# Tokens, stacks, probabilities and hidden rings at another place within 128 bytes of SBUF

## What is computed

```python
x = x + 0.5 * ffn(layernorm(x))
x = x + attn(layernorm(x))
x = x + 0.5 * ffn(layernorm(x))

# ffn: a gated layer of 1024 inner units, and 512 experts chosen by product keys
mlp = silu(x @ gate_w) * (x @ up_w) @ down_w
scores, pk = top_k(sx[:, :, None] + sy[:, None, :], 8)      # from top 8 of each of two key sets
ew = silu(x . down_embed[indices]) * softmax(scores)
out = mlp + ew @ up_embed[indices]

# attn: 16 heads of 16 features; q, k, v and o are linear layers with a low-rank update
scores = einsum('bhqd,bhkd->bhqk', q, k) / 4
out = lora_linear(einsum('bhqk,bhkd->bhqd', softmax(scores), v), Wo, ...)
```

## Time and profile before

| | |
|---|---|
| median of 3 runs | 810.65 us (809.98 to 813.35) |
| the profiled execution | 809.31 us, of which its span is 807.5 |
| PE busy | 788.1 us |
| VectorE busy | 659.9 us |
| ScalarE busy | 471.2 us |
| granted TensorE clock | 1.00 of full |

### The profile page before, as it was taken

One profiled execution on the slowest core, in us unless ns is written; L12 is line 12 of the kernel. 1 busy time (PEld: TensorE's weight loads), 2 busy tenths in 40 slices (PEclk: granted clock), 3 DMA queues, 4 the chain that ended last, 5 costly groups with the idle time before them and its releaser, 6 DMA issues.

```text
span 807.5 us, 14439 instructions
## 1 busy us (share of the span) xinstructions
PE 788.1 (98%) x5424; PEld 535.0 (66%) x5424; DVE 659.9 (82%) x1225; ACT 471.2 (58%) x929; POOL 155.4 (19%) x183
## 2 busy tenths in 40 slices
PE   5999999999999999999999999999999999999998
PEld 4778888887876544444444444444487888888886
DVE  5998788687779999999999999995078786775854
ACT  4544333333342699999999999999864342332323
POOL 1661102021111033332222222211100211020200
PEclk9999999999999999999999999999999999999999
DMA  8119000000040332223333222411000000000000
GB/s 286 40 40 409 8 1 2 1 1 0 1 79 14 65 57 41 41 41 93 93 93 94 41 41 43 125 69 68 2 2 0 1 2 27 0 27 1 1 26 27
DMA packets 18645, 40.45 MB, mean 50 GB/s; under 512 B 4688, under 2 KB 12176, under 8 KB 16528
## 3 DMA queue, kind: packets, MB, share of 16 engines
q1 hardware_dynamic: 18384, 39.14, 18.7%
q10 hardware_dynamic: 192, 0.39, 0.2%
HBM read 16.29 MB, written 10.49 MB: 33 GB/s over the span
## 4 chain that ended last, share of the span: by engine, by line
PE 92%; DVE 4%; issue 1%; ACT 1%; POOL 1%; DMA 1%; SPq 0%; DVEq 0%; ACTq 0%; POOLq 0%
PE front_ps L1560 17%; PE front_ps L1543 12%; PE max_ps L1503 9%; PE ffn_out_ps L659 6%; PE ffn_out_ps L661 5%; PE ffn_out_ps L660 5%; PE ffn_gate_ps L48 5%; PE ffn_gate_ps L50 5%; PE ffn_gate_ps L49 5%; PE ffn_up_ps L50 3%; PE ffn_up_ps L48 3%; PE ffn_up_ps L49 3%; PE ffn_mix_ps L643 2%; PE ffn_up_ps L379 1%; PE front_ps L1529 1%
## 5 line engine op out<-in xcount | busy, mean ns | idle before, releaser
L1713 DVE TENSOR_REDUCE maxima<-max_ps 128x1 f32<-128x512 f32 (+1 forms) x384 | 303.2, 859 | 6.3 <-PE max_ps L1503 5.3
L1651 ACT ACTIVATE probs<-front_ps 128x512 f32<-128x512 f32 x512 | 267.0, 598 | 27.1 <-PE front_ps L1543 22.8
L791 ACT ACTIVATE ffn_tanh<-ffn_gate_ps 128x512 f32<-128x512 f32 x96 | 57.5, 599 | 215.2 <-PE ffn_gate_ps L50 215.2
L1560 PE MATMUL front_ps<-probs,values 128*32 128x256 f32 x2048 | 150.1, 388 | 0.5 <-ACT probs L1651 0.4
L1037 DVE SCALAR_TENSOR_TENSOR ffn_gated<-ffn_tanh,ffn_gate_ps 128x512 f32<-128x512 f32 x96 | 65.7, 685 | 72.6 <-ACT ffn_tanh L791 72.6
L1560 PEld LDWEIGHTS front_ps<-probs,values 128*32 128x32 f32 x2048 | 47.0, 108 | 68.0 <-issue 55.6
L1461 POOL TENSOR_TENSOR inverse_sum<-turned,minus_one 128x16 f32<-128x16 f32 x15 | 43.7, 2915 | 241.5 <-ACT turned L1663 241.5
L1543 PE MATMUL front_ps<-q_stack,k_stack 49*128 49x512 f32 x256 | 86.6, 436 | 0.7 <-ACT attn_out L1269 0.7
L1503 PE MATMUL max_ps<-ffn_xlo,ffn_xhi 48*128 48x512 f32 x256 | 87.2, 437 | 0.0
L1543 PE MATMUL front_ps<-ffn_xhi,ffn_xlo 49*128 49x512 f32 x256 | 85.4, 444 | 0.0
L1503 PE MATMUL max_ps<-k_stack,q_stack 48*128 48x512 f32 x256 | 83.4, 447 | 0.0
(11 more groups left out here) (194 smaller groups left out, 1255.6 us busy)
## 6 DMA issues: line engine op xcount, KB each, us to landing
split_weights<-block SPq DMA_DIRECT2D x8, 1024.0 KB, 10.3
block<-split_weights SPq DMA_DIRECT2D x8, 1024.0 KB, 4.9
q_stack<-block SPq DMA_DIRECT2D x48, 64.0 KB, 2.3
ffn_xhi<-block SPq DMA_DIRECT2D x48, 64.0 KB, 2.3
ffn_xlo<-block SPq DMA_DIRECT2D x48, 64.0 KB, 2.3
k_stack<-block SPq DMA_DIRECT2D x42, 64.0 KB, 2.3
x_sb<-in_x SPq DMA_DIRECT2D x4, 512.0 KB, 6.3
out<-x_sb SPq DMA_DIRECT2D x3, 512.0 KB, 2.9
```

The lines of the kernel that those rows point to most:

```text
L1560: mm = pe.matmul(mixed_ps[strip:strip + STRIP, at:at + HALF // 2], values[g % SLOTS][:, kt, j, :], probs[:, (g * KEY_TILES + kt) % PROBS, ...
L1651: act.activation(probs[:, tile % PROBS, j, half * HALF:(half + 1) * HALF], score_ps[:, n % RING, :], ACT.Exp, scale=SCORE_SCALE).then_inc( ...
L1713: v.reduce_max(maxima[:, g % 2, m // 2, m % 2, heads], max_ps[:, m % 2, heads, :], axis=AXIS_X).then_inc(unit_max, 1)
```

## The change

It allocates two tiles that nothing reads or writes: 8 values (32 bytes) ahead of `ffn_xhi`, and in layer 1 alone 16 values (64 bytes) ahead of `hidden`. All that is allocated behind them moves by as much.

```diff
@@ -28,6 +28,8 @@
 CHUNKS = TOKENS // CHUNK
+HIDDEN_OFFSET = 16
+HALVES_OFFSET = 8
 CT = CHUNK // P
@@ -413,6 +415,8 @@
         full = sb("full", [P, 2, KT, PAIR_TILES, P])
+        if not first:
+            sb("beside_hidden", [P, HIDDEN_OFFSET])
         hidden = sb("hidden", [P, HIDDEN_RING, CHUNK])
@@ -1791,6 +1795,7 @@
         weights = FfnWeights(sem, blocks)
+        sb("beside_halves", [P, HALVES_OFFSET], F32)
         halves = [sb(f"ffn_x{i}", [P, KT, BATCH, SEQ], F32R) for i in ("hi", "lo")]
```

## The result

The changed kernel takes 817.72 us (median of 7, 814.71 to 819.34) against 810.65 for the kernel before (median of 7): a ratio of 1.0072, 95% interval 1.0052 to 1.0091. The forecast was 800.4, range 792 to 817. It is slower, and 0.7 us beyond the range.

A forecast was written before the change was run, and what follows sets the result against it. The prediction took the spacing of TensorE (PE) matmul starts to bound the kernel. Savings in both FFN layers, attention, projections and value rows sum to 10.3 us, from 810.65 to about 800.4 us; range 792 to 817.

The forecast's parts named there:

- What an address costs: Single-pass fp32r matmuls: a surcharge of 10 to 16 ns over 217 depends on the address; 223.3 ns forecast at 96.
- the line: fp32r passes: each 32 bytes of the stream's place modulo 128 are worth 3.3 ns, 223.3 at 96; chance 0.42.
- rival D: fp32r matmuls: the address surcharge is gone altogether, 217 ns a pass, 24 us saved, 787 us; chance 0.08.
- First layer: First FFN layer: 768 gate, up and down passes go from 226.7 to 223.3 ns, 2.6 us saved.
- Second layer: Second FFN layer: down passes save 2.9 us, gate and up 1.6, the gate products behind the downs 1.0.
- The 20 ns behind the down products: Second FFN layer: 20 ns extra in the six gate products behind each of 48 downs vanish, 1.0 us saved.
- Attention: Attention: 512 pairs of score and maximum matmuls save 3.3 ns each, 1.7 us, if pairs answer as single matmuls do.
- Projections and value rows: q/k projections save 0.3 us (96 x 3.3 ns), value rows 0.2 us (96 x at most 1.7 ns).
- C: Streams at 96 touch 33 pieces of 64 bytes instead of 32, 6.7 ns more a pass: 822 us; chance 0.08.
- B: Streams' last 128-byte block: its rest delays the next matmul, 96 costs 3.3 ns more than 64: 814.8 us; chance 0.13.
- A: Only the half of the 128-byte block counts, 96 behaves as 64; second FFN layer alone gains 2.9 us: 807.8; chance 0.23.
- E: Whole kernel: the change does not act, 6.7 ns belong to something else of the second FFN layer: 810.65 us; chance 0.06.

The follow-up runs named there:

- the kernel with blocks at 96: Changed kernel with its 32 bytes put ahead of block0 instead of ffn_xhi, so FFN weights stand at 96 too: 808.66 us, ratio 0.9964.
- the kernel at +128: Kernel before with tokens and both rings 128 bytes past the weights' place: 815.93 us, ratio 1.0045; 814.44 us at full clock.
- the kernel of sixteen pairs: Bare fp32r matmuls without the computation, weights and streams each at 0, 32, 64, 96 modulo 128: steady 228.6 and 229.1 ns for two pairs, 232.9 to 234.4 for fourteen.
- the two with one tile: Two kernels of bare fp32r matmuls without the computation, stepping the stream's distance from its weights: 237.2 ns at -16 in both.
- the ring alone moved: Kernel before with only 64 bytes put ahead of the second layer's hidden ring: 811.86 us, ratio 0.9993; 806.89 us in one execution at full clock.

## Why the prediction was wrong, point by point

**What bounds the kernel** was right: PE's spacing sets the time, and the loss lies in PE, with the other engines' work unchanged (ScalarE's tanh still takes 599 ns; VectorE in attention 281.39 of 318 us). Counts of passes and their lines were right as well, as was reading starts and not lengths.

**"What an address costs" is the step that failed.** It had three kinds of fp32r products: 64 on 64 at 226.7, 0 on 64 at 233.3, 64 on 0 at 228.8. I drew a line through the first two as if the weights, which stood at 64 in both, didn't matter, and wrote off the third as small. But the third is the one row in which weights stand elsewhere, and it has the stream at 64 and not the time of 64. By the stream's place the projections should have been at 226.7; they took 2.1 ns more, and this was in the earlier trace rows. The right reading of three rows was distances 0, -64 and +64, each with its own time, and +32 unknown. In the runs it is 233.3: 6.7 more, where the line gave 3.3 less. The remark that places relative to one another might count stood under rival D with the opposite sign, as a reason for the surcharge to vanish. "A loss by distance", in the same sentence, was the answer, and it got no case and no price.

**The terms.** First layer: forecast -2.6, came +3.3. At 6.7 ns each, 768 passes would be 5.1; but over the whole of the layer before the mean was not 226.7: it was 228.0 for gate, 227.0 for up and 228.8 for down passes (distances under 260 ns; after a change of kind some are uneven), and after is 233.0 to 233.1. These differences add up to 3.8 us; where the last 0.5 went is open. Second layer: forecast -5.5, came +1.65: gate from 230.4 to 233.3, up from 227.5 to 233.1, down 233.3 to 233.1. The 20 ns behind the down products did vanish as a step, but only because all three kinds take 233 ns now. Attention: forecast -1.7; its time did not change. The change leaves its distances at 0, and shifting only the stacks shows that pairs don't answer to 32 bytes either. Projections and value rows: -0.5, came 0; their distances (+64 and -64) are what they were. All else was costed at nothing, which held but for one wait of 0.9 us for a stack, in the profiled execution. Two readings were off without moving the forecast: 6.7 ns are 15 columns at the pace of rows 4 (0.443 ns each), not 16, and 0.11 us in the earlier trace rows is 3.5 ns over half of 213, not 6.

**The rivals.** C (6.7 ns more) has the right price in every FFN pass and the wrong reason: it rests on pieces of 64 bytes touched by a stream, and would have slowed the kernel with blocks at 96 just as much, which was faster. It also charged attention 3.4 us. B gave 814.8, and the changed kernel at full clock took 814.3 to 814.8, but that is chance: B has passes of 230 in all stages, and the trace has 233 in the FFN and no change elsewhere. A and E are refuted by the first layer alone, and D by the sign.

**The range** ended at 817 and the median is 817.72. The fall of the clock carries it over: it is in five of its seven executions. At full clock the kernel takes 814.79, and its second median was 815.80 (ratio 1.0061), both inside. So missing the range by 0.7 is in part chance; the wrong direction is not. I had read 1.00 in every stage of one execution and taken the clock as given, although the three times shown, 809.98 to 813.35, already had a spread of 3.4 us that I did not ask about.

**The two pages.** The formula of the Trainium skill ("TensorE: Matmul & The Clock Gate", Back-to-back issue gap), N / 2.4 + 2.5 ns or 215.8 for 512 columns, has no term for addresses; the section calls it the gap of a single matmul by itself. Full precision agrees with it at the one distance that was run, 0 modulo 256: 512 columns in two passes take 429 ns, 214.6 a pass. For fp32r it does not hold: 226.6 at best, 237.2 at worst. Lines of 16 bytes (the Trainium skill, "SBUF — State Buffer", Specifications) would give distance 128 the time of distance 0; the kernel at +128 is 4.9 us slower at full clock than before.

## What to carry to other kernels

Where fp32r matmuls of 512 columns run back to back and bound the time, keep the streamed operands and the loaded weights, those of neighbouring matmuls too, at the same byte place modulo 256, a multiple of 32: 226.7 ns instead of 233, here 807.6 us against 814.5 with the same instructions. Before moving a tile, list for each product the places of both operands; a time at two places of one operand says nothing on a third while the other operand stood still. Measure with one execution of bare matmuls over the distances in question, 12 of each: it costs less than arguing from a line through two points.

## What the runs showed that I had not expected

- The period is 256 bytes and the pattern is not monotonic: 226.6 at 0, 228.2 at 64, 231 to 235 at nearly all other multiples of 16, up to 237.2 at -16 and 236.8 at +4. Two results disagree: at -16 the kernel of sixteen pairs gave 226.4, the two with one tile 237.2. They differ in where the tiles lie and in the chip (the two that agree ran on two chips), and what of it matters is open.
- 512 columns answer, 128 don't, 256 answer in another order; pairs in two halves of the array don't, as far as 32 bytes show it. Full-precision matmuls took 429 ns in three kernels, but always at distance 0, so whether they answer was not tested.
- The granted clock fell to half for 6.8 or 10.2 us in the middle of dense PE work: in the 11.27 us before the fall shown above PE is busy 10.58. The rest is one wait for ScalarE that ends at 274.9 us, 2.3 us ahead of the fall. The kernel before, profiled without a fall, has the same wait at the same matmul (waiting instruction, what it waited for, total, times, longest; before, then after):

```profile
PE front_ps L1543 <- ACT attn_out L1269: 0.7, 1, 0.7
```
```profile
PE front_ps L1547 <- ACT attn_out L1273: 0.7, 1, 0.7
```

So neither what PE does there (projections, value rows, then pairs of few rows) nor this wait tells executions with and without the fall apart. The fall costs 3.7 us in the median of before (813.24 against 809.56) and 2.2 to 5.1 in the others. What makes it fall is not settled; that the changed kernel has it more often, 10 of 17 executions against 33 of 63, is no more than chance would give.
- It sets how finely such kernels can be compared: for the ring alone moved, nine executions of ten had the fall, and the median hid a gain of 2.7 us that the remaining one shows (806.89 against 809.56); one execution is no proof of its size.
